# Vision tower block, 16 images on one core: order of transfers and stages for the first five images

## The reference

```python
gray = einsum('bchw,c->bhw', x, (0.2989, 0.587, 0.114))
h = |conv(gray, scharr)|.sum(axis=1) / 2                     # 16 x 256 x 256
c_q, c_kv = ln(h) @ W_dq, ln(h) @ W_dkv                      # 256 -> 64
Q, K, V = c_q @ W_uq, c_kv @ W_uk, c_kv @ W_uv               # 16 heads of 16
attn = softmax(causal(Q K^T / 4));  h = h + (attn V) @ W_o
h = h + ln(h) @ sign(weight)^T
```

## Time and profile before

| | |
|---|---|
| median of 3 runs | 435.75 us (434.21 to 435.9) |
| the profiled execution | 436.89 us, span 435.1 us |
| TensorE busy | 368.5 us, 85% of the span |
| VectorE, ScalarE, GpSimd busy | 288.9, 238.9, 172.0 us |
| mean DMA rate | 170 GB/s, 74 MB moved |

### The profile page before, as it was taken

The page is one execution under the profiler, slowest core; times in us unless marked ns, Lnnn a source line. Parts: engine busy times, 40 slices in busy tenths (PEclk is TensorE's granted clock), DMA queues, the critical chain, the costliest instruction groups (busy, mean ns, idle before and its releaser), DMA issues.

```text
span 435.1 us, 9881 instructions
## 1 busy us (share of the span) xinstructions
PE 368.5 (85%) x3545; PEld 261.5 (60%) x3588; DVE 288.9 (66%) x539; ACT 238.9 (55%) x408; POOL 172.0 (40%) x367
## 2 busy tenths in 40 slices
PE   0335686999999999999999999999999989796764
PEld 0122364666676767676767676767676757574442
DVE  2224176886868687868686868686878776775520
ACT  2123425666767676767676767676757563534301
POOL 7032022545554546454545454545434323212200
PEclk9998669799999999999999999999999989898975
DMA  5966797959596878787878787675753534200000
GB/s 173 226 157 149 181 257 203 269 171 257 174 245 187 230 209 220 208 223 202 219 202 223 202 224 201 199 210 160 203 151 102 145 108 132 88 27 1 26 24 24
DMA packets 72266, 74.13 MB, mean 170 GB/s; under 512 B 6387, under 2 KB 66075, under 8 KB 72219
## 3 DMA queue, kind: packets, MB, share of 16 engines
q1 hardware_dynamic: 71355, 73.11, 61.5%
q10 hardware_dynamic: 864, 0.39, 0.3%
HBM read 51.98 MB, written 21.04 MB: 168 GB/s over the span
## 4 chain that ended last, share of the span: by engine, by line
PE 75%; DMA 7%; issue 5%; ACT 5%; DVE 4%; SPq 1%; POOL 1%; ACTq 0%; POOLq 0%
PE bank L910 14%; PE bank L1034 8%; PE bank L971 7%; PE bank L921 7%; PE bank L998 6%; PE bank L947 4%; PE bank L937 4%; PE bank L903 4%; PE bank L956 3%; PE bank L973 3%; PE bank L1037 3%; PE bank L1000 3%; PE bank L1015 3%; PE bank L984 3%; DMA q_st<-top_rows 3%
## 5 line engine op out<-in xcount | busy, mean ns | idle before, releaser
L628 ACT ACTIVATE probs<-bank 128x1024 f32<-128x1024 f32 x64 | 65.2, 1018 | 50.9 <-PE bank L1000 50.2
L774 DVE TENSOR_REDUCE top<-bank 128x4 f32<-128x1024 f32 x64 | 78.0, 1219 | 19.6 <-PE bank L973 19.5
L784 DVE TENSOR_TENSOR bank<-bank,cap_kq 128x512 f32<-128x512 f32 x64 | 44.7, 698 | 23.0 <-PE bank L1015 21.6
L971 PE MATMUL bank<-k_st,q_st 96*128 96x256 bf16 x256 | 48.3, 283 | 2.8 <-DMA k_st<-qk_parts 2.8
L921 PE MATMUL bank<-rows,band 102*32 102x256 f32 x512 | 34.1, 411 | 17.4 <-DMA rows<-gray_padded 17.4
L998 PE MATMUL bank<-q_st,k_st 99*128 99x256 bf16 x256 | 47.3, 278 | 1.0 <-DMA q_st<-top_rows 0.8
L1034 PE MATMUL bank<-probs,v_ring 128*32 128x256 f32 x512 | 42.4, 403 | 3.9 <-DVE rest L761 1.9
L779 DVE TENSOR_REDUCE top<-bank 128x4 f32<-128x512 f32 x64 | 41.6, 649 | 0.0
L471 POOL TENSOR_SCALAR var<-mv 128x2 f32<-128x2 f32 x16 | 3.6, 227 | 95.2 <-DVE mv L816 95.2
L633 ACT ACTIVATE probs<-bank 128x512 f32<-128x512 f32 x64 | 38.0, 594 | 3.8 <-DVE bank L784 3.6
L791 DVE STREAM_TRANSPOSE u<-bank 128x256 f32<-128x256 f32 x64 | 28.7, 448 | 11.1 <-PE bank L1037 5.9
(11 more groups left out here) (97 smaller groups left out, 750.9 us busy)
## 6 DMA issues: line engine op xcount, KB each, us to landing
x_sb<-in_x SPq DMA_DIRECT2D x16, 768.0 KB, 6.0
rows<-gray_padded SPq DMA_DIRECT2D x48, 256.0 KB
qk_parts<-parts SPq DMA_DIRECT2D x48, 256.0 KB, 3.1
q_st<-qk_parts SPq DMA_DIRECT2D x96, 128.0 KB, 3.0
k_st<-qk_parts SPq DMA_DIRECT2D x96, 128.0 KB, 3.0
gray_padded<-gray SPq DMA_DIRECT2D x16, 258.0 KB, 3.1
out_dram<-z SPq DMA_DIRECT2D x16, 256.0 KB, 3.0
rows<-gray_padded SPq DMA_DIRECT2D x32, 24.0 KB
```

What stands on the lines that cost most here:

```text
L628: nc.scalar.activation(probs[:, g, :, 0:S], ps_k0, ACT.Exp, scale=SCALE).then_inc(exp0_done, 1)
L774: nc.vector.tensor_reduce(top[:, 1, g // 2, :, g % 2], ps_hi, AX.X, ALU.max, negate=True).then_inc(max_hi_done, 1)
L784: nc.vector.tensor_tensor(ps_k1, ps_k1, cap_kq[:, :].unsqueeze(1).to_broadcast([P, G, P]), ALU.min).then_inc(capped, 1)
L971: nc.tensor.matmul(ps_hi[:, i, :], q[:, hh, P:S], k[:, hh, :], start=(i == b * two), stop=False, skip_group_check=True)
```

## The change

- **SyncE**: the turns before 1 are written out as one list. `load_operands(0, 0)` comes directly behind the stores of image 0, `load_rows(2)` and `load_rows(3)` come between and behind the operands of image 0, and `load_x(4)`, `load_x(5)` and `load_outputs` behind those of image 1. The five loads of projection weights and the three of ones move to ScalarE's queue. In every turn from 1 on, `load_x(i + 5)` stands behind `load_operands(i + 1)` where it stood ahead of it.
- **Layer norm of images 0 and 1**: `sum_and_scale` on VectorE adds the edges and measures them in halves and computes variance and shift; GpSimd keeps the power alone (`root_x`).
- **Parts of images 0 and 1** in halves, keys first: `second_part_halves` and `third_part_halves`.
- **TensorE**: `keep_warm(36)` ahead of the wait for the band, `keep_warm(10)` behind filters(0) and behind expand_v(0): bf16 products of constants, 512 columns each, into a PSUM bank not yet in use. filters(2) go from turn -1 into turn 0, into other banks. turn_x, compress and expand_qk of image 2 go from turn 0 into turn 1. The signs of the weight matrix are made and turned in turn 2 instead of 1.
- The lists of ScalarE, VectorE and GpSimd follow that order; gray of images 2 and 3 is made ahead of the parts of image 0.

```diff
             load_x(1)
-            for i in range(FIRST, LAST + 1):
-                if i == -4:
-                    store_gray(0)
-                    load_rows(0)
-                    load_projections()
-                    store_gray(1)
-                    load_x(2)
-                    load_rows(1)
-                    load_x(3)
-                    set_ones()
...
+            store_gray(0)
+            load_rows(0)
+            store_gray(1)
+            load_x(2)
+            load_rows(1)
+            load_x(3)
+            store_gray(2)
+            store_gray(3)
+            store_parts(0)
+            store_third(0)
+            load_operands(0, 0)
+            load_rows(2)
+            load_operands(0, 1)
+            load_rows(3)
+            store_parts(1)
+            store_third(1)
+            load_operands(1, 0)
+            load_operands(1, 1)
+            load_x(4)
+            load_x(5)
+            load_outputs()
+            for i in range(1, LAST + 1):
+                if live(i + 1):
+                    store_parts(i + 1)
+                if i == 1:
+                    store_gray(4)
+                if live(i + 1):
+                    store_third(i + 1)
+                if i == 1:
+                    load_rows(4)
+                if live(i + 1):
+                    load_operands(i + 1, 0)
+                    load_operands(i + 1, 1)
+                if live(i + 5):
+                    load_x(i + 5)
+                if live(i + 4):
+                    store_gray(i + 4)
...
             act.wait_ge(bordered, 1)
...
+            first_gray(0)
+            first_gray(1)
+            load_projections()
+            set_ones()
+            both_edges(0)
+            normalize_x(0)
+            first_gray(2)
+            copy_xt(0)
+            copy_c(0)
+            first_gray(3)
+            first_part(0)
+            second_part_halves(0)
+            both_edges(1)
+            copy_v(0)
+            normalize_x(1)
+            copy_xt(1)
+            copy_c(1)
+            first_part(1)
+            second_part_halves(1)
+            for i in range(LAST + 1):
...
+            def sum_and_scale(n):
+                for t in range(T):
+                    dve.wait_ge(abs_done, T * n + t + 1)
+                    nc.vector.tensor_tensor(h_ring[:, n % H_RING, t, :], edge[:, t, 0, :], edge[:, t, 1, :],
+                                            ALU.add).then_inc(h_done if t else top_h_done, 1)
+                    dve.wait_ge(h_done if t else top_h_done, n + 1)
+                    nc.vector.bn_stats(stats[:, t, :], h_ring[:, n % H_RING, t, :]).then_inc(stats_done, 1)
+                need(dve, xn_done, T * n)
...
+                nc.vector.tensor_scalar(var[:, :], mv[:, :, 1], EPS, None, ALU.add).then_inc(var_done, 1)
+                dve.wait_ge(rstd_done, n + 1)
+                nc.vector.scalar_tensor_tensor(shift[:, :], mv[:, :, 0], -1.0, rstd[:, :],
+                                               ALU.mult, ALU.mult).then_inc(shift_done, 1)
...
+            rest_of_gray(0)
+            rest_of_gray(1)
+            make_band()
+            make_up()
+            sum_and_scale(0)
+            rest_of_gray(2)
+            rest_of_gray(3)
+            rest_of_parts(0)
+            third_part_halves(0)
+            sum_and_scale(1)
+            rest_of_parts(1)
+            third_part_halves(1)
+            for i in range(LAST + 1):
...
+                if i == 1:
+                    measure_h(3)
+                    rest_of_parts(2)
...
+                if i == 1:
+                    turn_values(0, 0)
+                    rest_of_gray(4)
...
+            def keep_warm(count):
+
+                for _ in range(count):
+                    nc.tensor.matmul(bank[:, 5, :], ident_bf[:, :], mask_qk[:, :, :], start=True, stop=True)
+
             pe.wait_ge(drawn, 2 * TAPS + 5)
+            keep_warm(36)
             pe.wait_ge(band_ready, 1)
...
+                if i == 1:
+                    turn_x(2)
...
+                if i == 1:
+                    compress(2)
...
+                if i == -1:
+                    keep_warm(10)
 
...
+                if i == 1:
+                    expand_qk(2)
+                elif live(i - 1):
                     values(i - 1, 0)
                 if live(i):
                     hi_scores(i, 1)
                     lo_scores(i, 1)
+                if i == 1:
+                    values(0, 0)
+                    expand_v(2)
+                if i == 0:
+                    expand_v(1)
+                    filters(2)
+                    turn_max(0, 0)
...
-                if i == 1:
-                    pe.wait_ge(sign_ready, 1)
-                if live(i + 2):
+                if live(i + 2) and i:
                     expand_qk(i + 2)
-                if live(i + 3):
+                if live(i + 3) and i != -1:
                     filters(i + 3)
+                if i == -3:
+                    keep_warm(10)
```

More of the change, by code:

```diff
@@ L61 @@
 ON_VECTOR = 2
+BY_SCALAR = 5
 def live(n):
@@ new lines, in _ @@
+            load_x(4)
[17 more added lines that the diff above has]
+                    store_gray(i + 4)
+                if live(i - 3):
+                    store_z(i - 3)
+                if live(i + 4):
+                    load_rows(i + 4)
@@ L537, in _ @@
             pool.wait_ge(ones_set, 1)
-            for i in range(FIRST, LAST + 1):
+            for n in range(ON_VECTOR):
+                root_x(n)
+            for i in range(LAST + 1):
                 if live(i - 1):
                     cut_max(i - 1, 1)
+                if i == 0:
+                    cut_max(0, 0)
                 if live(i + 2):
@@ L548, in _ @@
                     third_part(i + 1)
-                if live(i):
+                if live(i) and i:
                     cut_max(i, 0)
@@ L562, in _, with load_projections, set_ones @@
         def _(act):
+            def load_projections():
+                act.dma_start(w_c[:, :, 0:DC], w_dq.rearrange("(t p) c -> p t c", p=P)).then_inc(weights_in, 16)
+                act.dma_start(w_c[:, :, DC:2 * DC], w_dkv.rearrange("(t p) c -> p t c", p=P)
+                             ).then_inc(weights_in, 16)
+                act.dma_start(raw_qk[0:DC, :], w_uq).then_inc(up_in, 16)
+                act.dma_start(raw_qk[DC:2 * DC, :], w_uk).then_inc(up_in, 16)
+                act.dma_start(w_v[DC:2 * DC, :], w_uv).then_inc(weights_in, 16)
+            def set_ones():
+                act.wait_ge(ones_drawn, 1)
+                for s in range(ST_RING):
+                    act.dma_start(k_st[KQ:KM, s, :, :, :].rearrange("p t h s -> p (t h s)"),
+                                 ones[:, :]).then_inc(ones_in, 16)
             def first_gray(n):
@@ L578, in both_edges @@
                     act.wait_ge(filters_done, T * n + t + 1)
-                    nc.scalar.activation(edge[:, t, :, :], ps_edge[:, t, :, :], ACT.Abs).then_inc(abs_done, 1)
+                    nc.scalar.activation(edge[:, t, :, :], (ps_edge2 if n == 2 else ps_edge)[:, t, :, :], ACT.Abs).then_inc(abs_done, 1)
             def normalize_x(n):
@@ L603, in first_part, with second_part_halves @@
                     nc.scalar.copy(parts[:, n % 2, 4 * i, :, :], ps_qk[i]).then_inc(part0_done, 1)
+            def second_part_halves(n):
+                for k, i in enumerate((1, 0)):
+                    act.wait_ge(rest_done, 2 * n + k + 1)
+                    nc.scalar.copy(parts[:, n % 2, 1 + 4 * i, :, :], rest[:, i, :, :]
+                                   ).then_inc(part1_done if k else key_part1_done, 1)
             def second_part(n):
@@ L671, in _ @@
                     exp_second(i - 1, 1)
-                if live(i + 4) and i > 0:
+                if i == 1:
+                    first_part(2)
+                    first_gray(4)
+                    second_part(2)
+                    copy_v(2)
+                    normalize_x(3)
+                if live(i + 4) and i > 1:
                     scale_colors(i + 4)
-                if live(i + 2):
+                if live(i + 2) and i > 1:
                     copy_xt(i + 2)
@@ L1116, in _ @@
                     lo_scores(i, 2)
+                if i == 1:
+                    turn_x(3)
                 if i == -2:
                     pe.wait_ge(weights_in, 3 * 16)
-                if live(i + 2):
+                if i == 2:
+                    pe.wait_ge(signed, 1)
+                    pe.wait_ge(v_copied, 4)
+                    turn(ps_w, signs, turned)
+                if live(i + 2) and i:
                     compress(i + 2)
```

156 lines of the change are left out of this document (62 added, 94 removed).

## The result

Over four runs of each, the median of the changed kernel is 446.95 us (445.59 to 448.57) against 435.82 us (434.21 to 438.86): a ratio of 1.0246, 95% interval 1.0203 to 1.0289. It is slower, where the prediction said faster, 429.7.

What follows compares the result with a forecast made beforehand. Bound: a head of some 93 us where TensorE starves or runs at half clock, then a TensorE-bound body. Lead 7.8 less 0.45 (signs) and 1.2 (late x) gains 6.1 us: 435.75 becomes 429.7, range 423.5 to 434.5.

Steps and rivals of the forecast that it cites:

- Turn 2 and later: Steady turns: from the 7.8 us lead, 0.45 lost for signs and 1.2 for late x, leaving 6.1 us.
- rival (4): Every turn: load_x behind load_operands, moved 10.9 us; landing beyond 9.4 us costs each of ten turns; 446 us, chance 0.09.
- Turn 0: First turn: its groups wait for VectorE's maxima; it ends at 56, six us before image 1's operands, hidden behind transfers.
- the idle stretch that I expected at 62: Before image 1's first scores: TensorE waits some 4 us for operands until 62, then half clock for 6 us.
- Head milestones: Head times: filters(0) at 18.7 us, x(3) by 28 to 29, image 0's stores at 32.4, load_operands(0, 0) at 36.1.
- rival (3): Head: weights on ScalarE's queue take turns with rows(0), which lands at 19 to 20.6; 431.6 us, chance 0.12.
- The 36 products: Head, ahead of filters(0): 14 constant products at 0.43 us and 22 at 0.22 take 10.8 us, ended at 18.9.
- The normalisation: Head, layer norm: the new form takes about 2.6 us instead of 4.8, saving 2.2.
- The short idle stretch before filters(4): End of turn 1: a second short TensorE idle near 83 us, as image 4's rows land at 83.2.
- Rival (1): Head: the lead of 12 us is kept because transfers keep up with the issue; 424.2 us, chance 0.18.
- Turn 1: Scores of image 1 at 62, half clock for 6 us, filters(4) last; turn 2 starts at 85.3, 7.8 us earlier.
- the sum of the transfers up to the parts of image 1: Head: 3.95 MB from 37.2 us at 222 GB/s take 17.8 us; parts land at 55.7, when load_operands(1, 0) issues.

Runs made afterwards that it cites:

- X_ahead: Changed kernel with load_x(i + 5) ahead of load_operands(i + 1) again from turn 2 on: 435.49 us, ratio 0.9986 to the kernel before.
- before_x_behind: Kernel before the change, with only load_x(i + 5) moved behind load_operands(i + 1) from turn 2 on: 449.32 us, ratio 1.0327.
- gray_then_x: Changed kernel with load_x(i + 5) put behind the operands, store_gray and store_z from turn 2 on: 442.0 us, ratio 1.0137.
- more_constants: x_ahead with 20 more constant products, 8 behind filters(0) and 12 behind the first scores of image 0: 432.44 us, ratio 0.9914.
- combined: x_ahead with weights and ones loaded on SyncE's queue again and 20 more constant products: 429.82 us, ratio 0.9872.
- gray3_behind: combined with gray of image 3 made and stored behind the parts of image 0 instead of ahead: 429.46 us, ratio 0.985.

## Why the prediction was wrong

**The step that failed** is "Turn 2 and later", with rival (4). The edit was named there, and so was the sign that would show it: "later turns of more than 22.3 us, or ScalarE waiting for x_sb". Its price was wrong: from the start of turn 2 I had 1.65 us lost (0.45 for the signs, 1.2 for x), and the profiled execution lost 11.9. The other 6.0 us of the miss are the head's (below). I followed the moved load to its own user, ScalarE, took it as moved by 10.9 us, and set the point from which it costs at 9.4 us of landing. I didn't ask what stands behind it in SyncE's queue. That is store_gray, whose landing SyncE waits for in line. In the kernel after, gray's landing went from 3.1 to 6.3 us and the parts' from 3.1 to 4.4 in the median; with the ring at 16.9 us against 21.67 there was room for 4.8 us. The turn read above needed 7.0 more: 3.7 for gray's landing, 2.0 for the parts', 0.8 for x, no longer issued under a landing, and 0.5 for slower issues. The result is 0.5 to 2.7 us in each of ten turns, 12.8 in all. X_ahead and before_x_behind show that the line causes it, in both heads; SyncE's waits show that the ring sets the turn, and gray_then_x that gray lands in 3.5 us once x is behind it. The late x of rival (4) appears too, but as a part of it: x was issued 6 to 8 us after expand_qk where it had been issued 10.4 ahead, 16 to 18 us later and not 10.9, since SyncE itself was late. The chance of 0.09 was for the right edit by the wrong mechanism, and the range left out its price.

**Turn 0 mis-sized.** Predicted 56 for its end; measured 65.8. I let the clock stay up after the first constant products. It didn't: the compression at 27.70 took 2.04 us, and filters(2) and filters(3) 3.64 each. In more_constants, where it stayed up, turn 0 ended at 59.1. Counted from the first scores of image 0, turn 0 took 20.1 us there, 15.0 in more_constants, and 14 in my sum. So some 5 of the 9.8 us are the clock, and 3.7 are the later start (45.72 against 42). This put turn 0 on the path: the operands for the first scores of image 1 had landed at 65.5, and the scores started at 68.21, without the idle stretch that I expected at 62.

**Head milestones late.** Filters(0) 20.09 against 18.7, wait for x(3) to 32.55 against 28 to 29, stores 36.5 against 32.4, load_operands(0, 0) 39.8 against 36.1. In combined, with the weights on SyncE, they are 17.46, 28.14, 32.10 and 35.38, near or ahead of what I wrote. So rival (3) held: TensorE waited for rows(0) until 20.09, within its 19 to 20.6, where I had put the cost at nothing. It was priced too low. I priced rows(0) alone, at up to 1.9 us; more came through store_gray(1), whose landing took 7.8 us and held x(3). The Trainium skill, "DMA: Bandwidth & Descriptors", "Queues, rings and completion order", would have it so: each DMA engine takes turns between the queues of SP and ACT. The trace agrees for rows(0): from 8 to 14 us ScalarE's queue moved 0.33 MB and SyncE's 0.66, where in combined SyncE's alone moved 0.93. For gray(1) it doesn't explain much: the five weights had landed by 13.73, and from 14 to 22 us ScalarE's queue moved 0.07 MB. How much of those 7.8 us belongs to rows(0) running late ahead of it, and how much to x(2) issued right behind it, no run tells apart.

**Right.** The 36 products took 10.8 us (7.67 to 18.45), as worked out. The normalisation took 2.45 us against 2.6. The short idle stretch before filters(4) came (1.28 us above). Rival (1), the lead kept, appears in no run.

**Right by luck.** Turn 1 took 23.1 us against 23.3, but not by its parts: the half clock that I put there was absent (the compression of image 2 took 1.13 us, not 2.05), and the rows of image 4 landed 4.7 us after their issue instead of 3. Combined starts turn 2 at 85.7, where I had 85.3, and measures 429.8, where I had 429.7. It takes three further edits to get there (x ahead again, the weights back, 20 more products), its turn 0 ends at 59.3 and not at 56, and my sum held 1.2 us for a late x that combined doesn't have. What it supports is the sum of the transfers up to the parts of image 1 (load_operands(1, 0) at 55.42, where I had 55.7), not the forecast. Some sums were also off in themselves: 37.2 + 17.8 is 55.0 and not 55.7, the upper bound of 59 is 55.9 by its own words (measured 59.46), 83.2 + 1.93 is 85.1, and from 75.29 to 81 us there are 5.7 us, not 6.3.

**Open.** Executions of x_ahead differ by 6.5 us (431.7 to 438.3), those of the kernel before by 3.7 beside them and by 6.9 beside the later runs (431.5 to 438.3). What makes the head vary wasn't found. What gray_then_x's first turns lose by is open too, and so is why gray lands in 4.6 us in x_ahead and in 3.1 in the kernel before.

## What to carry to other kernels

When a DMA is moved in an in-order queue, price it for its neighbours too: if a store that the queue later waits for stands behind it, the store can land later (here 6.3 us instead of 3.1). Sum the issuer's ring over one loop turn (issues plus every landing it waits for) and compare it with the compute bound; the difference, here some 4.8 us, is all that may be added. And measure a reordering of the head apart from the steady loop: here one line cost 2.6% in the body and hid what the head's edits did, part of them for and part against.

## What the hardware did that I had not expected

A 258 KB store that lands in 3.1 us took 6.3 us in the median, and 5.8 to 7.4 in the ten turns with a 768 KB load issued just ahead of it; with the load issued behind it, 3.5. And constant products ahead of the work lifted TensorE's clock for what came next, not dependably for what followed a wait: filters(0) took 1.93 us at 20.09, the full level of 2.4 GHz, but after the wait for the normalisation the compression at 27.70 took 2.04 us, the lower level of 1.2 GHz. With the same products it took 1.93 us in x_ahead and 1.19 in gray_then_x; with 8 more in that wait, 1.10 in more_constants, combined and gray3_behind. The 12 in turn 0 left filters(3) at 1.94 us in more_constants, but at 3.64 in combined and 3.48 in gray3_behind.
